# A Mamba layer with its feed-forward units: the skip term moves from VectorE into TensorE's sum, and the gated output overwrites z

## What is computed

```python
xc = silu(conv(xp) + b)                       # 256 channels, two blocks of 128
delta = softplus(dt @ Wdt + bdt)
h = exp(delta * A) * h + (delta * xc) * B     # 16 states a channel, along the tokens
y = sum_n(h * C) + xc * Dp                    # the skip term is xc * Dp
y = y * silu(z)                               # the gate
out = x + y @ Wblk
```

## Time and profile before

| what | us |
|---|---|
| median of three runs | 4566.4 |
| lowest and highest run | 4564.11 and 4567.35 |
| span of the profiled execution, first to last instruction | 4554.2 |
| busy time of GpSimd, VectorE, TensorE, ScalarE | 4093.5, 4047.9, 3939.2, 3342.2 |

### The profile page before, as it was taken

How to read it: one execution, slowest core, us unless ns; L and a number is a source line. 1 busy time by engine, 2 the same in 40 slices (tenths; PEclk the granted TensorE clock), 3 DMA queues, 4 the chain that set the end, 5 groups by cost and what they waited for, 6 DMA issues and landing times.

```text
span 4554.2 us, 48397 instructions
## 1 busy us (share of the span) xinstructions
PE 3939.2 (86%) x11712; PEld 1280.3 (28%) x11712; DVE 4047.9 (89%) x5505; ACT 3342.2 (73%) x5047; POOL 4093.5 (90%) x1804
## 2 busy tenths in 40 slices
PE   7886777998999999899998999999899989678769
PEld 2221222232322323232232323223232323122223
DVE  2668898999999999999999999999999999889963
ACT  4566776777777777777778777777777777667734
POOL 0559999999999999999999999999999999999960
PEclk9897887999999999999999999999999999789969
DMA  2233544354434444544454445444444554444410
GB/s 72 61 78 95 115 106 98 85 118 110 97 87 112 107 93 99 114 104 96 98 112 96 97 101 119 95 97 101 112 92 89 117 113 91 101 99 95 99 41 5
DMA packets 154562, 434.46 MB, mean 95 GB/s; under 512 B 16429, under 2 KB 53230, under 8 KB 153903
## 3 DMA queue, kind: packets, MB, share of 16 engines
q1 hardware_dynamic: 154287, 431.36, 41.4%
HBM read 150.28 MB, written 12.58 MB: 36 GB/s over the span
## 4 chain that ended last, share of the span: by engine, by line
POOL 41%; issue 16%; DVE 14%; PE 12%; ACT 8%; DMA 3%; SPq 2%; DVEq 0%; ACTq 0%; POOLq 0%
POOL work L909 21%; POOL work L900 19%; DVE work L720 5%; DVE dA_ps L720 4%; SPq L363 2%; PE d_ps L434 2%; PE s_ps L481 2%; DVE work L725 2%; DMA bc_sb<-bc_rows 2%; ACT sg_sb L583 2%; ACT L583 1%; PE b_ps L427 1%; ACT dA_ps L556 1%; DMA dd_sb<-dd_src 1%; ACT L584 1%
## 5 line engine op out<-in xcount | busy, mean ns | idle before, releaser
L909 POOL TENSOR_TENSOR work<-dd_sb,bc_sb 128x2048 f32<-128x2048 f32 x512 | 2319.6, 4531 | 72.4 <-DMA dd_sb<-dd_src 72.2
L556 ACT ACTIVATE dA_ps<-dd_sb,a_sb 128x512 f32<-128x512 f32 x2048 | 1369.2, 684 | 643.1 <-DVE work L725 542.9
L900 POOL TENSOR_TENSOR work<-work,bc_sb 128x1024 f32<-128x1024 f32 x704 | 1655.9, 2359 | 35.1 <-DVE work L720 34.7
L720 DVE TENSOR_TENSOR_SCAN work<-dA_ps,work 128x512 f32<-128x512 f32 x1408 | 1646.7, 1203 | 40.7 <-POOL work L909 32.0
L720 DVE TENSOR_TENSOR_SCAN dA_ps<-dA_ps,work 128x512 f32<-128x512 f32 x640 | 780.9, 1220 | 10.9 <-ACT dA_ps L556 5.1
L434 PE MATMUL d_ps<-sg_sb,wd_sb 128*128 128x512 f32 (+1 forms) x1536 | 721.0, 601 | 18.8 <-DVE sg_sb L805 18.8
L405 PE MATMUL y_ps<-work,sel_sum 128*32 128x512 f32 x4096 | 580.3, 640 | 81.9 <-POOL work L900 53.7
L421 PE MATMUL a_ps<-xT_sb,wg_sb 128*128 128x512 f32 (+1 forms) x768 | 439.5, 655 | 87.1 <-ACT sg_sb L583 80.7
L421 PE MATMUL b_ps<-xT_sb,wg_sb 128*128 128x512 f32 (+1 forms) x768 | 434.5, 648 | 92.2 <-ACT sg_sb L583 87.8
L725 DVE TENSOR_TENSOR work<-dA_ps,bc_sb 128x512 f32<-128x512 f32 x640 | 435.8, 681 | 8.3
L427 PE MATMUL a_ps<-xs_sb,wu_sb 128*128 128x512 f32 (+1 forms) x768 | 412.2, 619 | 20.7 <-DVE sg_sb L805 16.2
(11 more groups left out here) (116 smaller groups left out, 3823.6 us busy)
## 6 DMA issues: line engine op xcount, KB each, us to landing
dd_sb<-dd_src SPq DMA_DIRECT2D x512, 512.0 KB, 8.5
bc_sb<-bc_rows SPq DMA_DIRECT2D x256, 512.0 KB, 5.8
xr_sb<-in_L_attn_x SPq DMA_DIRECT2D x16, 256.0 KB, 3.3
bc_rows<-dbc_sb SPq DMA_DIRECT2D x128, 32.0 KB, 1.7
x<-xr_sb SPq DMA_DIRECT2D x16, 256.0 KB, 3.6
xr_sb<-x SPq DMA_DIRECT2D x16, 256.0 KB, 2.9
out<-xr_sb SPq DMA_DIRECT2D x16, 256.0 KB, 2.3
wg_sb<-in_L_ffn_Wg SPq DMA_DIRECT2D x1, 1376.0 KB
```

Source lines behind the costliest of these rows:

```text
L556: act.activation(dA_ps[:, g % NDA, :], dd_sb[:, b, c, 0, :], ACT.Exp, scale=a_sb[:, l, b, j, c:c + 1]).then_inc(dA_ready, 1)
L720: dve.tensor_tensor_scan(dA if on_dve(i) else tile, dA, tile, 0.0, ALU.mult, ALU.add).then_inc(scanned, 1)
L900: pool.tensor_tensor(work[:, g % RING], work[:, g % RING], bc_sb[:, j, 0, :].unsqueeze(1).broadcast_to([128, 2, T]), ALU.mult).then_inc(po ...
L909: pool.tensor_tensor(work[:, g % RING:g % RING + 2].rearrange("p h c t -> p (h c) t"), dd_sb[:, b, :, 1, :], bc_sb[:, j, 1, :].unsqueeze(1 ...
```

## The change

The skip term becomes a matrix product: for every layer and block a diagonal matrix of `Dp` is kept in SBUF, and TensorE opens each block's sum with the product of this diagonal and `xc`, into the whole bank, with the selection products accumulating on top. VectorE keeps the gate alone, and writes its result over silu(z). `y_sb` goes away. The tick tables are replaced by others.

```diff
-CORE = {"exp": -10, "scan": -1, "dbu": -3, "dve_prod": 0, "pool_prod": 21, "sum": 30, "y0": 87, "y1": 8}
-PREP = {"dc1": 79, "dc0": 65, "sq": -15, "ms": -10, "rms": -10, "xn": 2, "xp0": 15, "conv0": 17, "xp1": 25, "conv1": 25,
-        "silu_xc": 27, "z0": 35, "zc0": 27, "z1": 44, "zc1": 43, "silu_z": 59, "wx": 41, "dbc": 40, "rows": 4, "dt0": 48,
-        "sp0": 48, "delta0": 55, "du0": 59, "dt1": 75, "sp1": 72, "delta1": 79, "du1": 82, "dd0": 49, "dd1": 86, "bc": 52}
-NEAR = {"dc1": 98, "dc0": 84, "sq": 14, "ms": 25, "rms": 24, "xn": 27, "xp0": 45, "conv0": 42, "xp1": 47, "conv1": 53,
-        "silu_xc": 59, "z0": 69, "zc0": 60, "z1": 72, "zc1": 67, "silu_z": 91, "wx": 76, "dbc": 75, "rows": 48, "dt0": 77,
-        "sp0": 77, "delta0": 84, "du0": 84, "dt1": 84, "sp1": 86, "delta1": 93, "du1": 101, "dd0": 71, "dd1": 109, "bc": 55}
-POST = {"x1": 8, "wblk": 83, "h": 91, "attn": 105, "x2": 105}
-POST_NEAR = {"x1": -65, "wblk": 17, "h": 14, "attn": 35, "x2": 56}
+CORE = {"exp": -11, "scan": -1, "dbu": 2, "dve_prod": 2, "pool_prod": 24, "sum": 30, "y0": 88, "y1": 10}
+PREP = {"dc1": 84, "dc0": 64, "sq": -19, "ms": -6, "rms": -8, "xn": -4, "xp0": 15, "conv0": 8, "xp1": 20, "conv1": 25,
+        "silu_xc": 27, "z0": 95, "zc0": 91, "z1": 108, "zc1": 98, "silu_z": 123, "wx": 45, "dbc": 41, "rows": 39, "dt0": 46,
+        "sp0": 46, "delta0": 60, "du0": 62, "dt1": 73, "sp1": 71, "delta1": 78, "du1": 81, "dd0": 40, "dd1": 119, "bc": 80}
+NEAR = {"dc1": 95, "dc0": 80, "sq": 7, "ms": 25, "rms": 18, "xn": 26, "xp0": 47, "conv0": 49, "xp1": 56, "conv1": 56,
+        "silu_xc": 59, "z0": 109, "zc0": 104, "z1": 119, "zc1": 110, "silu_z": 123, "wx": 65, "dbc": 68, "rows": 12, "dt0": 76,
+        "sp0": 71, "delta0": 82, "du0": 82, "dt1": 83, "sp1": 84, "delta1": 90, "du1": 99, "dd0": 50, "dd1": 109, "bc": 44}
+POST = {"x1": -23, "wblk": 93, "h": 91, "attn": 104, "x2": 104}
+POST_NEAR = {"x1": -33, "wblk": 17, "h": 12, "attn": 28, "x2": 50}
...
+        APREP = 2 + 2 * NL + NL * NBLK
...
                     if j == 0 and 2 * k + b > 0:
                         pe.wait_ge(y_gated, 2 * k + b)
+                    if j == 0:
+                        pe.wait_ge(xc_ready, 2 * k + b + 1)
+                        pe.matmul(y_ps[:, :], ddiag_sb[:, PHASE[w][1], b, :], xc_sb[:, w % 2, b, :],
+                                  start=True, stop=False).then_inc(y_skip, 1)
                     for c in range(NG):
                         g = HALVES * k + 2 * u + c // 2
                         last = pe.matmul(y_ps[SEL * c:SEL * (c + 1), :], sel_sum[:, :], work[:, g % RING, c % 2, :],
-                                         start=(j == 0), stop=(j == NJ - 1))
+                                         start=False, stop=(j == NJ - 1))
...
-                        last = pe.matmul(ps[:, :], wblk_sb[:, PHASE[w][1], b, :], y_sb[:, b, :], start=(b == 0), stop=(b == NBLK - 1))
+                        last = pe.matmul(ps[:, :], wblk_sb[:, PHASE[w][1], b, :], zs_sb[:, w % 2, b, :], start=(b == 0), stop=(b == NBLK - 1))
...
-                            act.wait_ge(y_gated, 2 * (before - 1) + b + 1)
+                            act.wait_ge(wblk_full, before)
...
-                    act.wait_ge(aprep, 2 + 2 * NL)
+                    act.wait_ge(pprep, 3)
+                    for l in range(NL):
+                        for b in range(NBLK):
+                            act.activation(ddiag_sb[:, l, b, :], ident[:, :], ACT.Copy, scale=dp_sb[:, l, b:b + 1]).then_inc(aprep, 1)
+                    act.wait_ge(aprep, APREP)
...
                     dve.wait_ge(summed, UNITS * k + NJ * (b + 1))
-                    dve.scalar_tensor_tensor(y_ps[:, :], xc_sb[:, par, b, :], dp_sb[:, l, b:b + 1], y_ps[:, :],
-                                             ALU.mult, ALU.add).then_inc(y_skip, 1)
-                    dve.wait_ge(y_skip, 2 * k + b + 1)
                     dve.wait_ge(zs_ready, 2 * k + b + 1)
-                    if k > 0:
-                        dve.wait_ge(wblk_full, k)
-                    dve.tensor_tensor(y_sb[:, b, :], zs_sb[:, par, b, :], y_ps[:, :], ALU.mult).then_inc(y_gated, 1)
+                    dve.tensor_tensor(zs_sb[:, par, b, :], zs_sb[:, par, b, :], y_ps[:, :], ALU.mult).then_inc(y_gated, 1)
```

More of the change, by code:

```diff
@@ L45 @@
-END = {"yt": 21, "xo": 32, "bn": 41, "nb": 62, "xtok": 61, "ht": 84, "h": 74, "store": 133, "acc": 10}
+CORE = {"exp": -11, "scan": -1, "dbu": 2, "dve_prod": 2, "pool_prod": 24, "sum": 30, "y0": 88, "y1": 10}
+PREP = {"dc1": 84, "dc0": 64, "sq": -19, "ms": -6, "rms": -8, "xn": -4, "xp0": 15, "conv0": 8, "xp1": 20, "conv1": 25,
+        "silu_xc": 27, "z0": 95, "zc0": 91, "z1": 108, "zc1": 98, "silu_z": 123, "wx": 45, "dbc": 41, "rows": 39, "dt0": 46,
+        "sp0": 46, "delta0": 60, "du0": 62, "dt1": 73, "sp1": 71, "delta1": 78, "du1": 81, "dd0": 40, "dd1": 119, "bc": 80}
@@ L48, in phase_table @@
+FFN_AT = {"gb": 3, "xs": 4, "g0": 6, "g1": 8, "g2": 9, "burst": 5, "u0": 10, "u1": 11, "u2": 21, "hh0": 14, "hh1": 16,
+          "hh2": 22, "down": 29}
+START = {"load": -130, "bn": -60, "nb": -40, "xtok": -47, "xt": -33, "xT": -42, "lg": -29, "lg_sb": -37, "mx": -37,
+         "mi": -33, "gap": -15, "we": -29, "eq": -26, "den": -11, "inv": -27, "comb": -10, "ct": -16, "gates": -19}
+END = {"yt": 28, "xo": 34, "bn": 37, "nb": 52, "xtok": 50, "ht": 78, "h": 76, "store": 133, "acc": 17}
 def phase_table():
@@ L189, in build @@
         wblk_sb = sb("wblk_sb", [128, NL, NBLK, D])
+        ddiag_sb = sb("ddiag_sb", [128, NL, NBLK, 128])
         wout_sb = sb("wout_sb", [128, D])
@@ L222, in build @@
         sq_sb = xpad[:, KC - 1:]
-        y_sb = sb("y_sb", [128, NBLK, T])
         xr_sb = sb("xr_sb", [128, 2 * XSLOTS, TB, D])
@@ L534, in _ @@
                     pe.wait_ge(w_scan, 16 * SCAN_LOADS)
-                    pe.wait_ge(aprep, 2 + 2 * NL)
+                    pe.wait_ge(aprep, APREP)
                     pe.wait_ge(wconv_ready, 1)
@@ L733, in y_dve @@
                     k, w = at[:2]
-                    par, l = w % 2, PHASE[w][1]
+                    par = w % 2
                     dve.wait_ge(summed, UNITS * k + NJ * (b + 1))
-                    dve.scalar_tensor_tensor(y_ps[:, :], xc_sb[:, par, b, :], dp_sb[:, l, b:b + 1], y_ps[:, :],
-                                             ALU.mult, ALU.add).then_inc(y_skip, 1)
-                    dve.wait_ge(y_skip, 2 * k + b + 1)
                     dve.wait_ge(zs_ready, 2 * k + b + 1)
-                    if k > 0:
-                        dve.wait_ge(wblk_full, k)
-                    dve.tensor_tensor(y_sb[:, b, :], zs_sb[:, par, b, :], y_ps[:, :], ALU.mult).then_inc(y_gated, 1)
+                    dve.tensor_tensor(zs_sb[:, par, b, :], zs_sb[:, par, b, :], y_ps[:, :], ALU.mult).then_inc(y_gated, 1)
             def post_dve(t):
@@ L881, in _ @@
                     dve.wait_ge(w_scan, 16 * SCAN_LOADS)
-                    dve.wait_ge(aprep, 2 + 2 * NL)
+                    dve.wait_ge(aprep, APREP)
                     dve.tensor_tensor(wconv_sb[:, :, :, :], wconv_sb[:, :, :, :],
```

## The result

The changed kernel takes 4573.0 us, median of 20 runs (4569.4 to 4578.0), against 4567.7 for the kernel before in as many runs on the same chip: a ratio of 1.0014, 95% interval 1.0008 to 1.0021. That is 0.1% slower, where 46 us less were forecast. The profiled execution took 4573.9 us, 0.9 above the median.

What follows compares the result with a forecast made beforehand. GpSimd was taken to bound the middle, with late chains of short steps at the ends; 18 + 3 + 24 + 0 + 0.8 = 46 us off the 4566 median gives 4520 us, range 4494 to 4562.

Steps and rivals of the forecast that it cites:

- VectorE's relief: Skip term off VectorE shortens GpSimd's scan waits: 18 us in the middle, 3 outside it, 0.8 in the tail.
- The order of the middle: Middle phases: only shorter scan waits were counted as gain; the router's 16.6 us wait for the reciprocal was to stay.
- have no product between them in either table: GpSimd's two router steps around the reciprocal: given as the reason its 16.6 us wait stays.
- The product on TensorE: 128 diagonal products, 110 to 145 us of TensorE, to be covered by its idle time, mostly waits for silu.
- I count both at nothing: Diagonal products before units 0 and 4 of each sum: no cost on the path.
- TensorE too late: Rival: products at units 0 and 4 delay up matmuls, scans and GpSimd; 45 us lost in the middle, 4587; chance 0.12.
- a growing wait of L805 on TensorE: Sign of a wrong forecast: VectorE's up products wait over 0.7 us more per phase.
- Overwriting z: Gate writes over z: no instruction, and ScalarE's copy finds its wait for the output projection already met.
- The near starts: Eight late phase starts, from z's steps behind the delta chain: 3 us each, 24 us less (12 to 31.5).
- Removed, that is 4.15 us off the chain: Before the last phase, z's products and copies between silu and projection of xc: moving them saves 4.15 us.
- The head: Eight diagonal weights cost 3.0 us, z's move gives back 2.7: together taken as 0 (-2 to +4).
- The sum: Whole run: 18 + 3 + 24 + 0 + 0.8 = 46 us less, 4520 us; forecast chance 0.55.

Runs made afterwards that it cites:

- x6: Kernel before with the skip term left out on every engine, every tick as before: 0.9958 of before.
- x3: Changed kernel with four router ticks put back (gap behind product 14; logits, maxima, indices behind scan 29): 0.9983 of before, 4560.0 us.
- x18: x3 with four more START ticks as before or ahead of the down product (lg -32, xt -36, xtok -54, nb -44): 0.9982 of before.
- x7: x3 without the diagonal product, the skip term left out: 0.9978 of before, 4550.6 us.
- x13: x2 with the product in front of units 2 and 6 of the sum instead of 0 and 4: 1.0002 of before.
- x2: Kernel before, its own ticks, with the skip term as a product on TensorE (identity in place of the diagonal): 1.0000 of before.
- x16: Changed kernel with the overwriting undone (gated output in its own buffer, identity for the diagonal weights), no tick moved: 1.0173 of before.
- x1: Kernel before (skip term on VectorE, own buffer for the gated output) with every tick table of the changed kernel: 1.0195 of before.
- x12: Kernel before with five ticks moved: z's steps in near phases behind the delta chain: 1.0035 of before.
- x11: Kernel before with five ticks moved: z's steps in far phases at the changed kernel's places: 1.0283 of before.
- x4: Changed kernel with one tick moved: GpSimd's gap behind product 14 again, VectorE's logits still ahead of scan 29: 1.0032 of before.

## Why the prediction was wrong

- **VectorE's relief** (18 in the middle, 3 outside it, 0.8 in the tail: 22 us) measured 19 in x6. The size was right. Scan waits carry only part of it: they fell by 10.5 us, from 25.7 to 15.2, where 18 were forecast and under 10 named as the sign. Not seen was the gate's wait for the projection, 32 us, which opens as soon as the skip term no longer covers it.
- **The order of the middle** is the step that failed in the changed kernel: outside the near starts and the head the new tables were priced at nothing. The router was judged by one sentence, that GpSimd's two steps around the reciprocal "have no product between them in either table". That is so in both traces (after L939 comes L942 in all 32 routers of the changed kernel). But the wait there did not stay, it fell from 16.6 to 7.1 us, and the steps in front of it were not looked at: gap and indices went ahead of product 14, VectorE's logits ahead of scan 29, TensorE's transposes behind a down product. Four ticks of `START` take 14 us (x3 against the changed kernel; x18 has 15), and the rest of the new tables another 20 in the middle (x7 against x6), where GpSimd again waits in the router. Which ticks make those 20 stays open.
- **The product on TensorE**, "I count both at nothing", failed in the order of before. The rows gave 135 us of waits for silu, but at units 0 and 4 only 67.7 of them stood, against 83 us that 96 products need in phases 9 to 56 at the 0.86 of the earlier trace rows, and x13, with 63.5 at its units, cost the same. It cost 19 us there and took all of VectorE's gain (x2 against x6). This is the mechanism of the rival *TensorE too late*, at 19 where it had 45. Its sign, a growing wait of L805 on TensorE, came in x2 with 0.24 us per phase (103.8 us against 91.3) where 0.7 was named, and hardly in the changed kernel (93.8). In the order of the changed kernel, with four ticks put back, the product costs 2 us, 9 at most (x3 against x7); there "nothing" was nearly right.
- **Overwriting z** "takes no instruction": true, and its worth was missed. At the changed ticks it saves 73 us (x16), where the own buffer makes the gate wait for the projection. x1, with the changed ticks and the old buffer, has the same two waits (24.6 and 48.6 us).
- **The near starts** (8 times 3, 24 us): phases 0 to 4 and 57 to 63 took 20 us less in the pair of traces, and the waits for the DMA of delta, beside the first, went from 31.5 to 17.5 us (55.1 in eight places, the first 37.57). The size is near the forecast, but by luck, for z's move is not what brought it: alone it took 2 us off these waits (x12). The step that failed is "Removed, that is 4.15 us off the chain": removing one late step uncovered the transposes. In the changed kernel these moved too (`END`'s yt from 21 to 28), with much else, and the projection of xc starts with its silu, at 4325.14 after 4324.36. That yt is what did it was not tested by itself.
- **The head**: the eight diagonal weights took 2.43 us on ScalarE, 3.0 forecast, and VectorE's wconv waited 6.85 us instead of 4.35. The first phase began 0.7 us later in the pair of traces, but its start differs by up to 3 us between traces of the same head: 156.56 to 159.60 us in the five with that of before (before, x2, x6, x11, x13), 159.73 to 162.34 in the ten with that of the changed kernel. By their means it is 3.5 us, where 0 was forecast and -2 to +4 allowed.
- **The sum**: forecast 22 + 24 + 0 = 46 less. Step by step, by the ratios: from before to x6 19 less (VectorE's relief), to x7 9 more (the new tables, four ticks put back, with the overwritten buffer: by the two traces 21 less at the ends, 20 more in the middle, 7 more at the head and in phases 4 to 9), to x3 2 more (the product), to the changed kernel 14 more (the four ticks): 6 more in all, and the medians differ by 5. By way of x2 the product is 19 and the tables with the overwriting 6, so a price holds for its order of steps and the prices of two orders don't add up.

The rule that the prediction weighed, in the Trainium skill (Perfetto Trace Analysis, Identifying the Most-Contended Engine), is to optimise the engine of highest occupancy first. Read as the prediction read it, relieving VectorE gives the middle nothing; x6 took 19 us off the run, so this case's runs do not bear that reading out. Nor did the chain's shares tell the cost: x3 and x7 differ by 0.05% with 40% and 23% of TensorE on it. Here GpSimd's waits, and behind them the order in each queue, told where the time went.

Still open is why the product costs the same at either place tried in the order of before and almost nothing in the other, and which ticks lose the 20 us. The fastest kernels that compute all of it are x3 and x18, 0.998 of before.

## What to carry to other kernels

Idle time is cover only at the place where the new work stands: add up the waits there, not over the run, and then doubt them still, for x13's product left 10.7 us of the waits at its place unused and cost what it cost elsewhere. A price measured in one order of steps is no price in another: the product took 19 us with the tables of before and 2 with the new ones. When a change brings new orders for queues, read each queue's order around each cross-engine step, above all a step that waits with loop work behind it: one instruction two ticks too early cost 0.8% here, and half of a reordering (x4) was worse than none. And a buffer that is reused can be worth more for the wait that it takes away than for its room.

## What the runs showed of the hardware

GpSimd's two long instructions, the same in every kernel here, were not equally long in every trace. In the middle their groups read, in the changed kernel and then in x4, which differs by one tick and may have run on another chip:

```profile
L913 POOL TENSOR_TENSOR work<-dd_sb,bc_sb 128x2048 f32<-128x2048 f32 x414 | 1879.5, 4540 | 0.1
L904 POOL TENSOR_TENSOR work<-work,bc_sb 128x1024 f32<-128x1024 f32 x568 | 1339.9, 2369 | 15.0 <-DVE work L729 15.0
```

```profile
L913 POOL TENSOR_TENSOR work<-dd_sb,bc_sb 128x2048 f32<-128x2048 f32 x413 | 1871.6, 4532 | 0.1
L904 POOL TENSOR_TENSOR work<-work,bc_sb 128x1024 f32<-128x1024 f32 x567 | 1334.5, 2362 | 72.8 <-DVE work L729 72.7
```

Eight ns on 4532 and 7 on 2362 are 7 us over this stretch (414 x 8 + 568 x 7 ns), of the size of the whole result. The cause was not looked for.
